# Releasing a weight load by its buffer's last product and by GpSimd's count of scatters

## The chip, the cores and the metric

The kernel runs on one core of a Trainium2 chip. The metric is device time in microseconds (us) of one execution. Three runs of the kernel before took 980.37, 981.39 and 981.79 us, with a median of 981.39.

## The reference

A block of a transformer on 2048 rows of 512 numbers, in float32:

```python
x = x + attention(layernorm(x))   # linear attention, 16 heads of 128, running state
x = x + moe(layernorm(x))         # mixture of experts
```

The change lies in the experts. A classifier scores 64 choices for each row and keeps the best 8. Choices 32 to 63 carry no weights. For each of the 32 real experts, the rows that chose it go through

```python
gu = buf @ w_gate_up[e]           # 512 x 512
g, u = split(gu)
y = (silu(g) * u) @ w_down[e]     # 256 x 512
```

and each result, times the row's weight, is added to that row of the output.

## The kernel before, in words

The kernel has three stages in sequence: `attention`, `routing` (output projection, classifier, and a table of which rows each expert takes) and `experts`. `experts` begins at about 734 us in the profile.

**Weights.** One expert's weights are 1.5 MB, brought in by three DMAs of 512 KB each on SP's queue: the two halves of `w_gate_up` (parts 0 and 1, `load_up`, L1085) and `w_down` (part 2, `load_down`, L1090). A ring of eight buffers (`RING`, L1078) holds eight experts' raw weights; expert e uses buffer e % 8. Experts 0 to 7 are loaded in the stage before and at the start of this one, experts 8 to 31 by the loop at L1191. Products on TensorE are done in pairs of reduced precision, so ScalarE makes a high part of each weight tile (`split_high`, L1114, into `w_h`) and VectorE the rest (`split_low`, L1120, into a low buffer of the same ring place). Both run one to two experts ahead of the products: in step e of their loops (from L1365 and L1432) they split expert e + 2, and for expert e - 5's low part VectorE is therefore in its step e - 7.

**One expert.** GpSimd gathers its rows by an indirect DMA into `m_xg` (`gather`, L1213), two instructions of up to 128 rows each, six experts ahead; TensorE turns them (`turn`, L1254), makes the up product (`up`, L1268), turns the activation (`turn_a`, L1277) and makes the down product (`down`, L1290). In its step e it does `turn_a(e-1)`, `turn(e+1)`, `up(e)`, `down(e-1)` (L1306). ScalarE copies the result into `y`, which has four buffers (`weigh`, L1413); the copy for expert e waits until the scatter of expert e - 4 has landed (L1412). GpSimd adds `y` to the rows of `out` in memory by an indirect DMA (`scatter`, L1223).

**GpSimd's order.** Its loop (L1230) does for each e: the two gathers of expert e + 6 (each waits for VectorE's use of that buffer, L1210), then the scatter of expert e. A scatter waits for the output (L1222) and for the scatter of the expert before it to have landed (L1221). An expert with more than 64 rows has two scatters (the branch at L1237), another has one of 64 rows: 39 scatter instructions in all.

**SP's order.** SP issues loads strictly in order. Before each part of a load for expert e it waits, at L1194, for the last product that reads the buffer (up product of expert e - 8 for parts 0 and 1, its down product for part 2; semaphores `m_gu0`, `m_gu1`, `m_yd0`, `m_yd1`), and at L1195 for VectorE's low part of the same part of expert e - 5 (`m_wl`). After the last load it waits for all scatters (`m_s`, L1200).

`then_inc` raises a semaphore when an instruction is done (for a DMA, when the data has landed); `sem_inc` is an instruction of its own.

Of the kernel before, what the change touches and what calls it, by code (L numbers as in the profile page):

```python
# [1077 lines left out]
RING = 8  # L1078


def load_up(sm, eng, ring, wgu, e, halves=(0, 1)):
    up, _, _, _ = ring[e % RING]
    for i in halves:
        k = slice(2 * i, 2 * i + 2)
        eng.dma_start(up[:, k, :], wgu[e, k].rearrange("k p f -> p k f")).then_inc(sm[f"m_wg{e % RING}"], 16)  # L1085


def load_down(sm, eng, ring, wd, e):
    _, down, _, _ = ring[e % RING]
    eng.dma_start(down, wd[e].rearrange("k p f -> p k f")).then_inc(sm[f"m_wd{e % RING}"], 16)  # L1090
# [32 lines left out]
def experts(nc, sm, wgu, wd, xn2d, out, si, ring, consts, w_h, w_l, v_h):  # L1123


    with ExitStack() as ctx:
# [33 lines left out]
        def flags(eng, name):  # L1160
            return [eng.alloc_register(f"{name}{i}") for i in range(7)]
# [5 lines left out]
        def load_full(eng, regs, e):  # L1167
            eng.reg_load(regs[e % 7], full[0:1, 2 * e:2 * e + 1])  # L1168
# [13 lines left out]
        with nc.Block() as block:  # L1182
            @block.sync
            def _(eng):
                eng.dma_start(ident[:, :], consts[:, 0:128]).then_inc(sm["m_id"], 16)
                eng.wait_ge(sm["m_g01"], 16)
                load_up(sm, eng, ring, wgu, 6)
                load_down(sm, eng, ring, wd, 6)
                eng.wait_ge(sm["m_g11"], 16)
                load_down(sm, eng, ring, wd, 7)  # L1190
                for e in range(RING, NE):  # L1191
                    for part in range(3):
                        for t in range(2):
                            eng.wait_ge(sm[f"m_gu{t}" if part < 2 else f"m_yd{t}"], e - RING + 1)  # L1194
                        eng.wait_ge(sm["m_wl"], 3 * (e - RING + 3) + part + 1)  # L1195
                        if part < 2:
                            load_up(sm, eng, ring, wgu, e, (part,))
                        else:
                            load_down(sm, eng, ring, wd, e)
                eng.wait_ge(sm["m_s"], 32 * NE)  # L1200

            @block.gpsimd
            def _(eng):
                regs = flags(eng, "mp")

                def gather(e, t):

                    i = 2 * e + t
                    if e >= 6:
                        eng.wait_ge(sm[f"m_a{t}"], e - 5)  # L1210
                    else:
                        eng.wait_ge(sm["m_xg"], i + 1)
                    eng.indirect_dma_start(  # L1213
                        xg[:, e % 6, t, :], None, xn2d[:, :],
                        bass.IndirectOffsetOnAxis(ap=si[:, i:i + 1], axis=0),
                        bounds_check=T - 1, oob_is_err=False).then_inc(sm[f"m_g{t}{e % 6}"], 16)

                def scatter(e, t, rows, done):
                    i = 2 * e + t
                    if t == 0 and e >= 1:  # L1220
                        eng.wait_ge(sm["m_s"], 32 * e)  # L1221
                    eng.wait_ge(sm[f"m_y{t}"], e + 1)  # L1222
                    eng.indirect_dma_start(  # L1223
                        out[:, :], bass.IndirectOffsetOnAxis(ap=si[0:rows, i:i + 1], axis=0),
                        y[0:rows, e % 4, t, :], None, compute_op=ALU.add).then_inc(sm["m_s"], done)

                for e in range(6):
                    gather(e, 0)
                    gather(e, 1)
                for e in range(NE):  # L1230
                    if e + 6 < NE:
                        gather(e + 6, 0)
                        gather(e + 6, 1)
                    if e == 0:
                        eng.wait_ge(sm["m_full"], 1)
                    load_full(eng, regs, e)
                    with eng.If_lt(regs[e % 7], T):  # L1237
                        scatter(e, 0, P, 16)
                        scatter(e, 1, P, 16)
                    with eng.Else():  # L1240
                        scatter(e, 0, 64, 32)

            @block.tensor
            def _(eng):
# [197 lines left out]
def build(nc, x, wq, wk, wv, wo, wc, bias, wgu, wd, tabs, ca, cr, out):  # L1442
    with ExitStack() as ctx:
        sm = Sems(nc, ctx)
        oT = nc.dram_tensor("oT", [NC, P, NH, P], F32).ap()
        xn2d = nc.dram_tensor("xn2d", [T, XW], F32).ap()

        with nc.sbuf_tensor("v_h", [P, 24, 512], F32) as v_h, nc.sbuf_tensor("v_l", [P, 24, 512], F32) as v_l:
            pass
        w_h = ctx.enter_context(nc.sbuf_tensor("w_h", [P, 24, 512], F32R))  # L1450
        w_l = ctx.enter_context(nc.sbuf_tensor("w_l", [P, 24, 512], F32R))
        attention(nc, sm, x, wq, wk, wv, wo, tabs, ca, oT, w_h, w_l, v_h, v_l)
        si = ctx.enter_context(nc.sbuf_tensor("si", [P, 64], U32))
        with nc.sbuf_tensor("raw", [P, 18, 512], F32) as raw:
            pass
        low = ctx.enter_context(nc.sbuf_tensor("low", [P, 18, 512], F32R))
        ring = [(v[:, i:i + 4, :], v[:, i + 4:i + 6, :], w[:, i:i + 4, :], w[:, i + 4:i + 6, :])
                for v, w, n in ((raw, low, 3), (v_l, w_l, 4)) for i in range(0, 6 * n, 6)]
        ring7 = ring + [(v_h[:, 20:24, :], None, None, None)]
        routing(nc, sm, x, wo, wc, bias, cr, oT, xn2d, out, si, ring7, wgu, wd, w_h, w_l, v_h, v_l)  # L1460
        experts(nc, sm, wgu, wd, xn2d, out, si, ring, cr, w_h, w_l, v_h)
# [45 lines left out]
```

## Time and profile before

| | us |
|---|---|
| median of three runs | 981.39 |
| the profiled execution | 979.09 |
| its span, first to last instruction | 977.3 |

| engine | busy us | share of the span |
|---|---|---|
| TensorE, products (PE) | 902.5 | 92% |
| VectorE (DVE) | 772.9 | 79% |
| ScalarE (ACT) | 503.3 | 51% |
| GpSimd (POOL) | 482.5 | 49% |

The shares are means over three stages with different limits. The profile counts an instruction that issues an indirect DMA as busy while GpSimd writes its descriptors; the data moves afterwards. SP's DMA issues are listed as SPq, sequencer steps of GpSimd as POOLq.

### The profile page before, as it was taken

How to read it: one execution, taken by the hardware profiler on the slowest of the kernel's cores; microseconds unless marked ns; L12 is line 12 of the kernel's file. 1: busy time of each engine (PE TensorE's matmuls, PEld its weight loads, DVE VectorE, ACT ScalarE, POOL GpSimd, SP SyncE). 2: the span in 40 equal slices, each digit the busy share in tenths (PEclk: the TensorE clock that was granted, in tenths of full speed). 3: DMA queues.
4: the chain of work that ended last, by engine and by line, in shares of the span. 5: the costliest groups of instructions: out<-in, count | busy, mean ns of one | idle time of the engine just before them, and what ended most of it. 6: DMA issues, size and time to landing. Idle time of an engine off the chain costs nothing. (4 is left out here: it accounts for less than half of the span.)

```text
span 977.3 us, 14567 instructions
## 1 busy us (share of the span) xinstructions
PE 902.5 (92%) x4362; PEld 731.1 (75%) x4362; DVE 772.9 (79%) x1843; ACT 503.3 (51%) x867; POOL 482.5 (49%) x395
## 2 busy tenths in 40 slices
PE   4789999999999999999969999999976999998893
PEld 3577888888888888888848888888854677776672
DVE  6978888888888889888977777777776788887670
ACT  5455655555554655554563222332224687876671
POOL 2466766666766667766630000000006456775662
PEclk9999999999999999999999999999998999999897
DMA  8001111111111111110563676443155699999633
GB/s 309 6 33 49 51 46 50 59 45 49 39 59 50 44 59 51 39 59 35 195 224 145 209 266 208 148 148 119 56 192 185 162 331 323 293 299 279 201 43 43
DMA packets 67368, 127.06 MB, mean 130 GB/s; under 512 B 12072, under 2 KB 14504, under 8 KB 65232
## 3 DMA queue, kind: packets, MB, share of 16 engines
q1 hardware_dynamic: 58144, 114.67, 33.7%
q0 software_dynamic: 9136, 11.31, 6.2%
q8 instruction: 43, 0.70, 0.3%
q14 instruction: 45, 0.37, 0.1%
HBM read 106.53 MB, written 32.90 MB: 143 GB/s over the span
## 5 line engine op out<-in xcount | busy, mean ns | idle before, releaser
L595 POOL TENSOR_TENSOR a_t<-a_t 128x512 f32<-128x512 f32 x80 | 105.1, 1314 | 99.0 <-DVE a_t L358 99.0
L604 POOL TENSOR_TENSOR a_fQ<-a_fQ,a_den 128x512 f32<-128x512 f32 x64 | 88.0, 1375 | 71.8 <-DVE a_den L396 71.8
L213 PE MATMUL a_PQ<-w_h,a_xT_h 128*128 128x512 f32 x384 | 106.9, 400 | 10.1 <-DVE w_l L345 9.4
L782 PE MATMUL r_PY<-w_h,r_o_h 128*128 128x512 f32 x256 | 105.9, 414 | 3.4 <-DVE r_o_l L884 3.4
L1070 POOL TENSOR_SCALAR r_vr<-r_mv 128x1 f32<-128x1 f32 x16 | 8.4, 525 | 196.6 <-DVE r_mv L895 196.6
L213 PE MATMUL a_PQ<-w_l,a_xT_h 128*128 128x512 f32 x384 | 104.5, 395 | 0.0
L213 PE MATMUL a_PQ<-w_h,a_xT_l 128*128 128x512 f32 x384 | 103.4, 391 | 0.0
L782 PE MATMUL r_PY<-w_h,r_o_l 128*128 128x512 f32 x256 | 101.0, 395 | 0.0
L1223 POOL DMA_INDIRECT out<-m_y,si x39 | 69.1, 1772 | 64.5 <-DMA out<-m_y,si 51.2
L782 PE MATMUL r_PY<-w_l,r_o_h 128*128 128x512 f32 x256 | 100.5, 393 | 0.0
L392 DVE CUSTOM_DVE_ANT_0 a_m<-a_fQ,a_z 128x128 f32<-128x128 f32 x256 | 100.4, 445 | 0.0
L1213 POOL DMA_INDIRECT m_xg<-xn2d,si x64 | 79.0, 1235 | 39.5 <-DVE m_xg L1340 18.2
L611 POOL TENSOR_TENSOR a_A_l<-a_A,a_A_h 128x512 fp32r<-128x512 f32 x64 | 89.0, 1391 | 6.5 <-ACT a_A_h L480 6.5
L213 PEld LDWEIGHTS a_PQ<-w_h,a_xT_h 128*128 128x128 f32 x384 | 70.0, 190 | 25.3 <-issue 11.2
L357 DVE TENSOR_TENSOR a_t<-a_PQ,a_tab 128x512 f32<-128x512 f32 x80 | 55.0, 688 | 41.7 <-PE a_PQ L213 41.7
L213 PEld LDWEIGHTS a_PQ<-w_l,a_xT_h 128*128 128x128 f32 x384 | 73.2, 191 | 15.8
L494 ACT ACTIVATE a_t<-a_t 128x512 f32<-128x512 f32 x80 | 50.0, 625 | 67.4 <-POOL a_t L595 67.2
L213 PEld LDWEIGHTS a_PQ<-w_h,a_xT_l 128*128 128x128 f32 x384 | 72.9, 190 | 15.4
L480 ACT ACTIVATE a_QT_h<-a_PT 128x512 fp32r<-128x512 f32 x64 | 38.1, 596 | 80.7 <-PE a_PT L221 80.7
L1120 DVE TENSOR_TENSOR w_l<-v_l,w_h 128x1024 fp32r<-128x1024 f32 x48 | 57.2, 1222 | 5.7 <-ACT w_h L1114 4.3
L782 PEld LDWEIGHTS r_PY<-w_h,r_o_h 128*128 128x128 f32 x256 | 48.5, 189 | 12.0 <-issue 3.8
L782 PEld LDWEIGHTS r_PY<-w_h,r_o_l 128*128 128x128 f32 x256 | 48.5, 189 | 11.2
(182 smaller groups left out, 2245.3 us busy)
## 6 DMA issues: line engine op xcount, KB each, us to landing
oT<-a_o SPq DMA_DIRECT2D x64, 256.0 KB, 2.4
v_l<-in_wgu SPq DMA_DIRECT2D x32, 512.0 KB
raw<-in_wgu SPq DMA_DIRECT2D x24, 512.0 KB
v_l<-oT SPq DMA_DIRECT2D x11, 1024.0 KB, 7.2
v_l<-in_wd SPq DMA_DIRECT2D x16, 512.0 KB
raw<-in_wd SPq DMA_DIRECT2D x12, 512.0 KB
v_h<-oT SPq DMA_DIRECT2D x5, 1024.0 KB, 6.9
out<-r_x SPq DMA_DIRECT2D x18, 256.0 KB, 2.0
```

Of the source, the lines that this page charges most:

```text
L213: last = eng.matmul(bank[:, :], a[:, k, :], w[:, 4 * i + k, :], start=s == 0 and k == 0, stop=s == 2 and k == 3)
L357: eng.tensor_tensor(heads(t1[:, r % 2, :]), q, spread(tab[:, c % 2, 0, :]), ALU.mult)
L392: last = eng.tensor_tensor_reduce(m[:, cols], fQ[:, n % 3, cols], z[:, c % 2, g * P:(g + 1) * P], 1.0, 1e-6, ALU.mult, ALU.add, den[:, n % ...
L480: eng.activation(out, in_, ACT.Copy).then_inc(sm[kind], 1)
L494: eng.activation(t2[:, r % 2, :], t1[:, r % 2, :], ACT.Relu, scale=-1.0).then_inc(sm["r"], 1)
L595: eng.tensor_tensor(t1[:, r % 2, :], t1[:, r % 2, :], t2[:, r % 2, :], ALU.add).then_inc(sm["xr"], 1)
L604: eng.tensor_tensor(q, q, den[:, n % 2, :].unsqueeze(2).broadcast_to([P, 4, P]), ALU.mult).then_inc(sm["fs"], 1)
L611: eng.tensor_tensor(A_l[:, n % 2, :], A[:, n % 2, :], f(A_h[:, n % 2, :]), ALU.subtract).then_inc(sm["Al"], 1)
L782: last = eng.matmul(PY[c % 2][:, :], a[:, c % 2, h * P:(h + 1) * P], b[:, h, :], start=h == 0 and s == 0, stop=h == NH - 1 and s == 2)
L1120: eng.tensor_tensor(low, src, high.bitcast(F32), ALU.subtract).then_inc(sm["m_wl"], 1)
L1213: eng.indirect_dma_start(xg[:, e % 6, t, :], None, xn2d[:, :], bass.IndirectOffsetOnAxis(ap=si[:, i:i + 1], axis=0), bounds_check=T - 1, o ...
L1223: eng.indirect_dma_start(out[:, :], bass.IndirectOffsetOnAxis(ap=si[0:rows, i:i + 1], axis=0), y[0:rows, e % 4, t, :], None, compute_op=AL ...
```

## The change

SP no longer waits for VectorE's low part of expert e - 5. From expert 10 on it waits instead until a new semaphore, `m_sent`, has reached e - 9. GpSimd raises `m_sent` by one, by an instruction of its own behind the scatter (or the two scatters) of each expert, so e - 9 is reached behind the scatter of expert e - 10. The waits for the buffer's last product stay.

```diff
                     for part in range(3):
                         for t in range(2):
                             eng.wait_ge(sm[f"m_gu{t}" if part < 2 else f"m_yd{t}"], e - RING + 1)
-                        eng.wait_ge(sm["m_wl"], 3 * (e - RING + 3) + part + 1)
+                        if e >= RING + 2:
+                            eng.wait_ge(sm["m_sent"], e - RING - 1)
                         if part < 2:
                             load_up(sm, eng, ring, wgu, e, (part,))
                         else:
...
                     with eng.If_lt(regs[e % 7], T):
                         scatter(e, 0, P, 16)
                         scatter(e, 1, P, 16)
+                        eng.sem_inc(sm["m_sent"], 1)
                     with eng.Else():
                         scatter(e, 0, 64, 32)
+                        eng.sem_inc(sm["m_sent"], 1)
```

## Rows read from the trace of the kernel before

**Rows 1.** The page, the chain that ended last: shares of the span by line.
```profile
POOL out L1223 1%; POOL m_xg L1213 1%; DMA m_xg<-xn2d,si 1%; PE m_PG L1268 0%; POOLq L1168 0%; POOLq L1182 0%; PE m_PX L1254 0%; DVE m_a L1331 0%; ACT m_s L1401 0%; POOLq L1237 0%; POOLq L1222 0%; POOLq L1213 0%
```

**Rows 2.** The waits, 780 to 880 us: us in total, times, longest us.
```profile
POOL out L1223 <- DMA out<-m_y,si: 20.6, 12, 4.1
```

**Rows 3.** Windows: length, busy us and instructions by engine, TensorE clock, DMA share, GB/s.
```profile
745.00:768.00 23.00, 17.20 (x75) 13.27 (x74) 14.27 (x19) 9.80 (x17) 13.11 (x12) 0.85 0.45 117
780.00:800.00 20.00, 19.11 (x87) 14.05 (x88) 17.62 (x23) 17.40 (x27) 10.96 (x8) 1.00 1.01 334
780.00:880.00 100.00, 95.82 (x449) 73.72 (x450) 84.37 (x106) 82.47 (x126) 69.39 (x45) 1.00 0.98 311
920.00:945.00 25.00, 25.00 (x128) 21.00 (x127) 18.90 (x26) 18.73 (x31) 17.04 (x13) 1.00 0.36 58
```

**Rows 4.** The waits, 880 to 945 us.
```profile
PE m_PX L1254 <- DMA m_xg<-xn2d,si: 6.6, 3, 4.0
```

**Rows 5.** Timeline of POOL, scatters: start us, us, instruction, idle before and its releaser.
```profile
774.41 1.62 POOL L1223 DMA_INDIRECT out<-m_y,si  x1 [5.17 <-ACT m_y L1413]
...
784.95 1.67 POOL L1223 DMA_INDIRECT out<-m_y,si  x1 [4.12 <-DMA out<-m_y,si]
...
804.23 1.47 POOL L1223 DMA_INDIRECT out<-m_y,si  x1 [1.14 <-DMA out<-m_y,si]
...
811.69 1.89 POOL L1223 DMA_INDIRECT out<-m_y,si  x1 [2.83 <-DMA out<-m_y,si]
...
824.06 2.29 POOL L1223 DMA_INDIRECT out<-m_y,si  x1 [0.91 <-DMA out<-m_y,si]
...
831.12 2.22 POOL L1223 DMA_INDIRECT out<-m_y,si  x1 [2.12 <-DMA out<-m_y,si]
...
843.16 1.94 POOL L1223 DMA_INDIRECT out<-m_y,si  x1 [0.30 <-issue]
...
853.54 1.47 POOL L1223 DMA_INDIRECT out<-m_y,si  x1 [2.08 <-DMA out<-m_y,si]
...
860.42 1.99 POOL L1223 DMA_INDIRECT out<-m_y,si  x1 [1.90 <-DMA out<-m_y,si]
...
871.37 2.20 POOL L1223 DMA_INDIRECT out<-m_y,si  x1 [0.74 <-DMA out<-m_y,si]
...
882.25 1.51 POOL L1223 DMA_INDIRECT out<-m_y,si  x1 [2.47 <-DMA out<-m_y,si]
...
895.70 1.63 POOL L1223 DMA_INDIRECT out<-m_y,si  x1 [2.03 <-DMA out<-m_y,si]
...
905.14 1.48 POOL L1223 DMA_INDIRECT out<-m_y,si  x1 [1.68 <-DMA out<-m_y,si]
...
923.93 1.87 POOL L1223 DMA_INDIRECT out<-m_y,si  x1 [2.56 <-DMA out<-m_y,si]
...
950.15 1.76 POOL L1223 DMA_INDIRECT out<-m_y,si  x1 [2.40 <-DMA out<-m_y,si]
...
957.56 1.43 POOL L1223 DMA_INDIRECT out<-m_y,si  x1 [3.77 <-DMA out<-m_y,si]
...
969.18 1.43 POOL L1223 DMA_INDIRECT out<-m_y,si  x1 [2.40 <-DMA out<-m_y,si]
```

**Rows 6.** Timeline of ACT, outputs of experts 5 and 31.
```profile
796.83 0.60 ACT L1413 ACTIVATE m_y<-m_PY 128x512 f32<-128x512 f32 x1
...
962.53 0.60 ACT L1413 ACTIVATE m_y<-m_PY 128x512 f32<-128x512 f32 x1 [2.20 <-PE m_PY L1290]
```

**Rows 7.** Timeline of SP, up loads of experts 8, 18 and 19.
```profile
768.41 1.50 SPq L1085 DMA_DIRECT2D raw<-in_wgu  x2
...
823.94 1.50 SPq L1085 DMA_DIRECT2D raw<-in_wgu  x2
...
832.09 1.50 SPq L1085 DMA_DIRECT2D v_l<-in_wgu  x2
```

**Rows 8.** Timeline of PE, last up product of expert 0.
```profile
746.81 1.07 PE L1268 MATMUL m_PG<-w_h,m_xT_l 128*128 128x512 f32 x4
```

**Rows 9.** The chain in order of time: start us, us, what.
```profile
957.33 0.30 POOLq L1168
```

## The prediction, made before the change was run

> **What bounds the kernel now.** Read the chain of waits first. It names GpSimd's scatter to `out` (L1223) and its gather into `m_xg` (L1213) ahead of everything else, TensorE only behind them [rows 1]. So the expert stage ends on GpSimd, and the waits say what holds GpSimd: between 780 and 880 us its scatters waited 20.6 us, in 12 waits, for the scatter before them to land [rows 2]. `scatter` asks for that (L1221). The windows give the reason: the 16 DMA engines are 98% to 101% busy from 780 to 880 us, at 311 to 334 GB/s, and at 36% and 58 GB/s once the weight loads are over [rows 3]. TensorE waits later, and for GpSimd: 6.6 us in three waits for gathered rows [rows 4].
>
> Now follow GpSimd's scatters [rows 5]. Expert 5's starts at 804.23, expert 22's at 923.93: 17 steps in 119.70 us. Three steps hold two scatters (experts 11, 15, 18: 843.16 to 853.54, 871.37 to 882.25, 895.70 to 905.14: 10.38 + 10.88 + 9.44 = 30.70). The other 14 take 89.00, or 6.36 each. Without loads, from expert 28 to 31, a step takes (969.18 - 957.56) / 3 = 3.87. GpSimd also falls behind: the output of expert 5 is ready at 796.83 + 0.60 = 797.43 [rows 6] and goes out at 804.23; that of expert 31 is ready at 963.13 [rows 6] and goes out at 969.18, 6.05 later.
>
> Last, SP's load issues [rows 7]. Loads are never late for their readers: ScalarE's splits do not appear among the long waits. What a load does to the time is what it does to the scatter beside it.
>
> **The change, part by part.** *Removed:* 72 waits on VectorE's low-part count (3 for each of 24 experts). They paced a load to VectorE's work on the expert five back, whatever GpSimd was doing. What is left of the old condition, the last product out of the buffer, allows expert 8's load when expert 0's second up product is done, at 746.81 + 1.07 = 747.88 [rows 8], where it went at 768.41 [rows 7]: 20.5 us earlier for its first two parts, into a stretch whose DMA engines are 45% busy [rows 3]. The third waits for expert 0's down product as before. I price this by the first step that it uncrowds, expert 1's two scatters to expert 2's, 774.41 to 784.95: 10.54, with 4.12 of waiting at its end [rows 5]. Bounds: 10.54 (no gain), and the two-scatter step without loads, 950.15 to 957.56 = 7.41 (gain 3.13). I take 1.0, near the first end, because loads of experts 9 and 10 still lie beside that step.
>
> *Added on GpSimd:* 32 counts. They are sequencer steps. The step behind a scatter runs at 957.33, before the scatter itself starts at 957.56 [rows 5, 9]: the sequencer passes a scatter as its wait ends, and the count will too, about 0.23 before the scatter starts rather than behind it. The cost is nothing as long as a scatter of 1.43 us or more hides it. Uncovered, at the 0.30 of that step, it would be 32 x 0.30 = 9.6 us.
>
> *Added on SP:* 66 waits (22 experts, three parts). Behind them on SP stand only later loads and the final wait. A load can't become late: `y` has four buffers, ScalarE's copy waits for the scatter four back (L1412), so GpSimd is at most some four experts behind, and a load freed by the scatter ten back still has about four of TensorE's steps before its split. Cost nothing.
>
> *Moved:* from expert 5 or so on, GpSimd's lag (6.8 us there) is more than one step of TensorE, so the count, not the product, comes last. Each load then goes out once per GpSimd step, its first DMA about 0.15 us before a scatter starts (an estimate: the 0.23, less the hop to SP), the other two behind it; SP's issue of two takes 1.50 us [rows 7]. Its bytes are the same, and so is the number of loads between the scatters of experts 5 and 22: 17, one per step. So only their place against the scatter matters.
>
> Its price isn't in the trace; I bound it. Each 512 KB DMA that gets ahead of a scatter costs it 0.524 MB / 334 GB/s = 1.57 us [rows 3]. A step without loads is 3.87. One DMA ahead gives 5.44, two give 7.01. Rows agree with both ends: expert 8's scatter at 824.06, with the load's first DMA 0.12 before it (823.94), made a step of 7.06 to 831.12. Six steps whose load began 0.35 to 0.97 after the scatter (experts 6, 7, 9, 10, 13, 14, of which 832.09 behind 831.12 is one) took 12.37 + 12.04 + 10.95 = 35.36, or 5.89 each [rows 5, 7]. The new place lies between these two patterns: the first DMA is surely ahead, the second is issued just before the 1.43 us of the scatter's own instruction end, the third behind. I take one and a half: 3.87 + 1.5 x 1.57 = 6.22. Against 6.36 that is 14 x 0.14 = 1.9 us.
>
> The two-scatter steps I leave as they are; with loads (10.23 on average) and without (7.41) they differ by 2.8 each, 8.5 in all, which the range takes in. The tail behind expert 22 has no loads in either kernel: 0.
>
> **Sum.** 1.0 + 1.9 = 2.9 us off the profiled execution's 979.09 (span 977.3 and 1.8 around it): 976.2. The median of the runs, 981.39, is 2.3 above that execution, so I predict 978.5. About 0.2% (2 us) is what a measurement of this kernel can tell from no change.
>
> **Floor.** However fast GpSimd becomes, TensorE's chain stays. GpSimd can gain its 6.05 us of lag at the end and TensorE's 6.6 of waiting for rows [rows 4]: 12.7 us, 968.7.
>
> **Rivals.**
> *The scatter keeps ahead.* Steps fall to the 5.89 of the six rows: 14 x 0.47 = 6.5, with the start 7.5 us: 973.9. For it: regular spacing, so that the load before is done when the next begins. Against: the load still goes out before the scatter, which those six did not. Chance 0.30.
>
> *The load gets ahead.* The count is raised as the scatter leaves its wait, SP issues two DMAs before the scatter's own data moves, and every step becomes like expert 8's. Place: the scatter's wait on the scatter before. Price: 14 x (7.01 - 6.36) = 9.1 less 1.0, so slower by 8.1: 989.5. It decides once the second DMA's data precede the scatter's. For it: the 7.06 row, and the 0.23. Against: it is one row, and that scatter's instruction took 2.29 us where a lone one takes 1.43 [rows 5], so that more could slip ahead of it. Chance 0.18.
>
> *Place does not matter.* If the engines served a scatter the same whether a load was issued before or behind it, steps would stay at 6.36, and the start alone would count: 1.0 us off, 980.4. Against: with one load beside each, steps took 5.89 in one pattern and 7.06 in the other. The Trainium skill, page "DMA: Bandwidth & Descriptors", section "Queues, rings and completion order", speaks for this rival and so against the change: each DMA engine takes turns between its queues' rings, packet by packet, so that an earlier issue holds no place in a common line. The two patterns, 1.17 us apart, do not bear that out. Chance 0.08.
>
> *The count is never last*, because GpSimd keeps up: then loads merely go a step earlier, hidden as before: 981.4. The 6.8 us lag is against it. Chance 0.04.
>
> **How the numbers follow.** The forecast, steps of about 6.05 to 6.40, has 0.40: some 975.5 to 981, rather more of it below 979.4 than above (0.25 and 0.15). Faster: 0.25 + 0.30 = 0.55. Within 0.2%: 0.15 + 0.08 + 0.04 = 0.27. Slower: 0.18. The range, 970 to 987, holds the forecast, the rivals at 973.9 and 980.4, and steps up to some 6.8; it leaves out the full price of two DMAs ahead, and gains near the floor.
>
> **What would show it.** In the changed kernel: expert 8's load near 748; from about expert 15 on every load's first DMA 0.1 to 0.7 us before GpSimd's scatter of the expert ten back; steps between scatters more even, near 6.2, and less than 20.6 us of scatter waits from 780 to 880; fewer of TensorE's waits for rows near 890 to 910; last scatter about 3 us earlier, with the same steps of 3.87 behind expert 28. Steps near 7 with more waiting for landings would prove me wrong on the sign, steps near 5.9 on the size. Loads that follow VectorE or TensorE instead of GpSimd's scatters would show that the count isn't what releases them.

## The result, and the profile of the changed kernel

| | before | after |
|---|---|---|
| median of five runs, us | 980.95 | 1000.93 |
| the profiled execution | 979.09 | 996.43 |
| its span | 977.3 | 994.5 |

The ratio is 1.0202, with a 95% interval of 1.0171 to 1.0234: slower, by some 2%, against a forecast of 978.5 and outside its range. The profiled execution is the fastest of the five; what follows is compared with the 977.3 of the span before.

Begin with GpSimd's scatters in the timeline of the changed kernel (start, duration, idle before and its releaser), the rows that answer to [rows 5]: experts 5, 11, 12, 14, 15, 16, 18, 19, 22, 25, 28 and 31. The scatter is now line 1224.

```profile
809.14 2.42 POOL L1224 DMA_INDIRECT out<-m_y,si  x1 [3.51 <-DVE m_a L1334]
...
852.65 1.97 POOL L1224 DMA_INDIRECT out<-m_y,si  x1 [2.87 <-DMA out<-m_y,si]
...
863.57 1.47 POOL L1224 DMA_INDIRECT out<-m_y,si  x1 [3.35 <-DMA out<-m_y,si]
...
876.92 1.48 POOL L1224 DMA_INDIRECT out<-m_y,si  x1 [1.56 <-DMA out<-m_y,si]
...
883.91 2.48 POOL L1224 DMA_INDIRECT out<-m_y,si  x1 [2.10 <-DMA out<-m_y,si]
...
894.13 1.48 POOL L1224 DMA_INDIRECT out<-m_y,si  x1 [2.17 <-DMA out<-m_y,si]
...
909.09 2.55 POOL L1224 DMA_INDIRECT out<-m_y,si  x1 [2.30 <-DMA out<-m_y,si]
...
919.65 1.48 POOL L1224 DMA_INDIRECT out<-m_y,si  x1 [1.68 <-DMA out<-m_y,si]
...
941.36 1.47 POOL L1224 DMA_INDIRECT out<-m_y,si  x1 [2.83 <-DMA out<-m_y,si]
...
956.75 1.65 POOL L1224 DMA_INDIRECT out<-m_y,si  x1 [0.30 <-issue]
...
974.54 1.42 POOL L1224 DMA_INDIRECT out<-m_y,si  x1 [3.35 <-DMA out<-m_y,si]
...
986.26 1.43 POOL L1224 DMA_INDIRECT out<-m_y,si  x1 [2.41 <-DMA out<-m_y,si]
```

From expert 5 to expert 22 the 17 steps take 941.36 - 809.14 = 132.22 us, where they took 119.70. The three steps with two scatters take 10.92 + 10.22 + 10.56 = 31.70 (before 30.70); the 14 single ones 100.52, or 7.18 each (before 6.36). Expert 22 to 31 takes 44.90 (before 969.18 - 923.93 = 45.25). So 12.52 of the 17.2 us arise between experts 5 and 22, none in the tail. The other 4.91 are there at expert 5 already, and 2.50 of those before the first weight split of the stage, which started later in this execution (ScalarE's timeline, the kernel before and the changed one):

```profile
716.07 1.99 ACT L1114 ACTIVATE w_h<-raw 128x1024 fp32r<-128x1024 f32 x2
```

```profile
718.57 1.99 ACT L1114 ACTIVATE w_h<-raw 128x1024 fp32r<-128x1024 f32 x2
```

SP's timeline of the changed kernel shows expert 8's load and, for a step in the middle, expert 24's, which is released by the count behind expert 14's scatter:

```profile
752.57 0.88 SPq L1085 DMA_DIRECT2D raw<-in_wgu  x2
...
876.78 0.88 SPq L1085 DMA_DIRECT2D raw<-in_wgu  x2
877.77 0.41 SPq L1090 DMA_DIRECT2D raw<-in_wd  x1
```

Expert 24's first DMA goes 0.14 us before the scatter at 876.92, its second 0.47 and its third 0.99 behind the first. All three are issued before the scatter's own instruction ends, at 876.92 + 1.48 = 878.40. From expert 15's load on that is so in 15 of 17 steps; in the steps of experts 6 and 8 the third DMA goes as the instruction ends or just behind. In the kernel before, the same two up DMAs took 1.50 [rows 7], not 0.88.

What SP waited for in the changed kernel, 780 to 945 us (us in total, times, longest), shows that the count is what releases the loads:

```profile
SPq L1196 <- POOLq L1244: 91.1, 16, 9.4
SPq L1196 <- POOLq L1241: 16.4, 3, 5.5
```

Next, which bytes move in that step. The DMA view gives packets, MB and share of the engines for each kind of queue: hardware_dynamic holds SP's loads, software_dynamic GpSimd's gathers and scatters. First the changed kernel from 878 to 881 us, then from 881 to 883:

```profile
q1 hardware_dynamic: 478, 0.95, 88.4%
...
q1 hardware_dynamic: 281, 0.54, 72.2%
q0 software_dynamic: 77, 0.13, 35.0%
```

For three microseconds only the load moves, though the scatter's descriptors were written by 878.40. Behind 881 come 0.13 MB of GpSimd's, which is the size of this scatter (64 rows of 2 KB); it lands in time for the next to start at 883.91. Of the load's 1.57 MB, 0.95 go before the scatter's rows and the last of it beside them (0.54 MB between 881 and 883). Where no load is in the way, a scatter's rows move sooner: those of expert 28's, issued at 974.54, between 976.4 and 978 (the DMA view of that stretch):

```profile
q0 software_dynamic: 80, 0.13, 67.0%
```

That is up to 3.5 us behind the scatter's start, where the one at 876.92 has its rows 4.1 to 6.1 us behind it.

The waits of the changed kernel, 780 to 880 and then 880 to 945 us, answer to [rows 2, 4]:

```profile
POOL out L1224 <- DMA out<-m_y,si: 30.9, 12, 4.6
...
PE m_PX L1257 <- DMA m_xg<-xn2d,si: 6.0, 2, 5.3
...
PE m_PX L1257 <- DMA m_xg<-xn2d,si: 10.5, 5, 5.0
ACT m_y L1416 <- DMA out<-m_y,si: 9.9, 3, 5.1
```

Scatters wait 30.9 us for landings where they waited 20.6. GpSimd falls so far behind that others wait for it earlier: TensorE for gathered rows in both stretches (10.5 us in the second, before 6.6), ScalarE's copy for the scatter four back. The windows answer to [rows 3]:

```profile
780.00:880.00 100.00, 90.06 (x409) 68.86 (x409) 78.48 (x98) 75.62 (x113) 57.11 (x41) 0.97 0.85 264
920.00:945.00 25.00, 24.31 (x112) 20.05 (x113) 18.15 (x24) 18.23 (x30) 14.44 (x12) 0.91 0.79 242
```

The DMA engines are 85% busy from 780 to 880 us where they were 98%, and loads still run behind 920 us, where they had run out before. In the kernel before, the engines were full in that stretch; this one is held by a circle: a scatter waits for a load, the next load waits for the next scatter, and the engines idle in between.

### The profile page after: what moved, and what is told of

Read it like the earlier page. It is cut to its first block and busy times, and to the rows that moved or that the text cites. A ratio compares the mean times of both kernels' runs of the same rounds, so it can differ in the third digit from the quotient of the medians.

```text
span 994.5 us, 14599 instructions
## 1 busy us (share of the span) xinstructions
PE 906.7 (91%) x4362; PEld 735.9 (74%) x4362; DVE 773.5 (78%) x1843; ACT 503.7 (51%) x867; POOL 480.1 (48%) x395
## 5 line engine op out<-in xcount | busy, mean ns | idle before, releaser
L1224 POOL DMA_INDIRECT out<-m_y,si x39 | 64.2, 1647 | 80.7 <-DMA out<-m_y,si 64.0
L1214 POOL DMA_INDIRECT m_xg<-xn2d,si x64 | 81.8, 1278 | 40.0 <-DVE m_xg L1343 18.0
L213 PEld LDWEIGHTS a_PQ<-w_h,a_xT_h 128*128 128x128 f32 x384 | 70.1, 190 | 25.4 <-issue 11.3
```

Of the source, the lines that this page charges most:

```text
L213: last = eng.matmul(bank[:, :], a[:, k, :], w[:, 4 * i + k, :], start=s == 0 and k == 0, stop=s == 2 and k == 3)
L1214: eng.indirect_dma_start(xg[:, e % 6, t, :], None, xn2d[:, :], bass.IndirectOffsetOnAxis(ap=si[:, i:i + 1], axis=0), bounds_check=T - 1, o ...
L1224: eng.indirect_dma_start(out[:, :], bass.IndirectOffsetOnAxis(ap=si[0:rows, i:i + 1], axis=0), y[0:rows, e % 4, t, :], None, compute_op=AL ...
```

## The experiments

Theory A: the time follows the number of load DMAs issued ahead of a scatter's own descriptors. Rivals: B, the tie to GpSimd itself, since it lets loads go later; C, the three DMAs come as a burst now that VectorE doesn't pace them, wherever the burst stands; D, late loads starve the splits; E, below.

### None ahead

A small write by GpSimd's engine behind the scatter raises the count, in place of the sequencer's step. `tick` has a column for each expert and is read by nothing. The edit is the same in both branches; one is shown, here and below.

```diff
-                        eng.sem_inc(sm["m_sent"], 1)
+                        eng.memset(tick[:, e:e + 1], 0.0).then_inc(sm["m_sent"], 1)
```

> Edit: the count is raised by a small memset of GpSimd's engine behind the scatter instead of by its sequencer, so that it rises when the scatter's descriptors have been written (some 1.6 us after the scatter's start) and not 0.14 us before it. Everything else is as in the changed kernel. Theory A (three load DMAs issued just ahead of each scatter hold up its landing): the three DMAs are issued at about +1.6, +2.1 and +2.6 us, behind the scatter's own data; the landing is then held by nothing, single steps between scatters fall from 7.18 us towards the 5.3 of the one step of the kernel before whose loads came at +1.72, and the time falls by 14 x (1.3 to 1.9) = 18 to 27 us, to 974 to 983. Theory B (the tie to the scatter itself, which lets loads go late, costs the time): loads go 1.7 us later still, so 1000 or a little more. Theory C (the loads are no longer spaced by VectorE, and a burst of three DMAs in 1 us takes the engines from gathers and scatters wherever it stands): the burst is as dense, so 996 to 1003.

Measured: 974.08 us, ratio to the kernel before 0.9922 (0.9891 to 0.9953). That is 27 us below the changed kernel, with the same releases, some 1.8 us later. Between the two profiles' spans lie 23.4 us: 12.71 in the 14 single steps from expert 5 to 22, 5.82 in the three steps with two scatters, 7.43 before expert 5's scatter, and 2.69 the other way behind expert 22's. The timeline of this kernel around expert 10's scatter, GpSimd first, then SP:

```profile
835.18 1.47 POOL L1225 DMA_INDIRECT out<-m_y,si  x1 [2.40 <-DMA out<-m_y,si]
836.15 0.62 POOL L1245 MEMSET m_tick<- 128x1 f32 x1
...
840.38 1.63 POOL L1225 DMA_INDIRECT out<-m_y,si  x1 [0.30 <-issue]
...
836.85 0.90 SPq L1085 DMA_DIRECT2D v_l<-in_wgu  x2
837.85 0.41 SPq L1090 DMA_DIRECT2D v_l<-in_wd  x1
```

The load goes 1.67 us behind the scatter's start, just behind its end at 836.65. The DMA view of this kernel, 837 to 838.5 and then 839 to 842 us:

```profile
q0 software_dynamic: 75, 0.12, 74.8%
q1 hardware_dynamic: 46, 0.09, 26.2%
...
q1 hardware_dynamic: 555, 1.08, 99.9%
```

Now the scatter's bytes move first and the load's behind them. In the window from 780 to 880 us TensorE is busy 95.66 us again (90.06 in the changed kernel), and the DMA engines 97% (85%):

```profile
780.00:880.00 100.00, 95.66 (x449) 73.90 (x448) 84.79 (x106) 82.89 (x125) 70.34 (x62) 1.00 0.97 293
```

Theories B and C fall as they stand: the tie is the same, the burst is the same (three DMAs within 1.0 us). Single steps took 6.27, not the 5.3 that I expected at best.

### One ahead, two ahead

Both keep the sequencer's count for the first DMA or the first two, and wait for a second semaphore, `m_tick`, raised as above, for the rest. With one ahead:

```diff
-                            eng.wait_ge(sm["m_sent"], e - RING - 1)
+                            eng.wait_ge(sm["m_sent" if part == 0 else "m_tick"], e - RING - 1)
```

With two:

```diff
-                            eng.wait_ge(sm["m_sent"], e - RING - 1)
+                            eng.wait_ge(sm["m_sent" if part < 2 else "m_tick"], e - RING - 1)
```

> Edit: the first of a load's three DMAs waits for the sequencer's count (0.14 us ahead of the scatter), the other two for a count raised by a memset behind the scatter (some 1.6 us after its start). Theory A: one DMA of 0.524 MB instead of three stands ahead of each scatter, so about a third of the way from the kernel with all three behind to the changed one: 982 to 990. Theory B: 998 to 1003. Theory C: the burst is cut in two, 975 to 990, and the same as or faster than the kernel with all three behind.

Measured: 978.85 us, ratio 0.997 (0.994 to 1.000), a little below what A gave.

> Edit: the first two of a load's three DMAs wait for the sequencer's count (ahead of the scatter), the third for a count raised by a memset behind the scatter. Theory A (the time follows the number of load DMAs ahead of the scatter): none ahead gave 974.1, one 978.9, three 1000.9; two lie between, 985 to 994; the rival of the prediction priced two ahead at 989.5. Theory A2 (a threshold: TensorE and the scatters hide one DMA, and any more stands in full): 988 to 1001. Theory C (the density of the burst costs the time): 975 to 982, since the burst is cut in two as with one ahead.

Measured: 990.18 us, ratio 1.0074 (1.0048 to 1.0101). That is in A's span, but also in that of A2, the threshold, so this run does not part the two. From none to three ahead the medians rise by 4.8, 11.3 and 10.8 us: the first DMA costs less than each of the others. SP's timeline with two ahead, beside expert 8's scatter:

```profile
833.69 1.48 POOL L1225 DMA_INDIRECT out<-m_y,si  x1 [1.65 <-DMA out<-m_y,si]
...
833.55 0.88 SPq L1085 DMA_DIRECT2D raw<-in_wgu  x2
835.37 0.37 SPq L1090 DMA_DIRECT2D raw<-in_wd  x1
```

### The write alone

Theory E: the small write helps by itself. Here it stands behind the scatter but raises nothing, and the sequencer's count stays.

```diff
                         eng.sem_inc(sm["m_sent"], 1)
+                        eng.memset(tick[:, e:e + 1], 0.0)
```

> Edit: the changed kernel with its sequencer count, and the same small memset behind the scatter as in the fast kernels, which here raises nothing. Theory A (the place of the loads against the scatter's own descriptors costs the time, and the memset matters only as a later signal): loads stay 0.14 us ahead of a scatter, 996 to 1004. Theory E (the memset itself helps, by holding GpSimd's engine behind the scatter): 970 to 985.

Measured: 999.52 us, ratio 1.0202 (1.0117 to 1.0286). E falls; the write matters as a later signal only.

### The sequencer's count behind the gathers

```diff
                         gather(e + 6, 1)
+                    if e >= 1:
+                        eng.sem_inc(sm["m_sent"], 1)
...
-                        eng.sem_inc(sm["m_sent"], 1)
```

> Edit: the sequencer's count, as in the changed kernel, but raised behind the next expert's two gathers instead of right behind the scatter, with no instruction of GpSimd's engine added. The loads then go some 3 to 4 us behind a scatter's start and 1.5 to 3 us ahead of the next one, so that a part of their 4.7 us still stands ahead of that next scatter. Theory A (what counts is the bytes of load still unfinished ahead of a scatter): better than three DMAs just ahead of it, worse than right behind the last one: 977 to 990. Theory A' (it is the order within the GpSimd queue alone, any place behind the scatter is as good): 970 to 977. Theory D (the sequencer's count is the trouble by itself, wherever it stands): 995 or more.

(D is here another theory than the D above.) Measured: 991.33 us, ratio 1.0092 (1.0054 to 1.013), between A's span and D's. D falls by the kernel with one ahead, which has the sequencer's count too and took 978.85. But the loads did not stand where I had put them. The timeline, the scatters of experts 8 to 10 with the gathers between the first two, and SP's issues behind expert 8's below:

```profile
829.34 1.48 POOL L1224 DMA_INDIRECT out<-m_y,si  x1 [0.56 <-DMA out<-m_y,si]
831.13 1.77 POOL L1214 DMA_INDIRECT m_xg<-xn2d,si  x1 [0.30 <-issue]
833.21 1.00 POOL L1214 DMA_INDIRECT m_xg<-xn2d,si  x1 [0.30 <-issue]
835.28 1.93 POOL L1224 DMA_INDIRECT out<-m_y,si  x1 [1.07 <-DMA out<-m_y,si]
...
842.63 2.09 POOL L1224 DMA_INDIRECT out<-m_y,si  x1 [2.78 <-DMA out<-m_y,si]
...
830.27 0.89 SPq L1085 DMA_DIRECT2D raw<-in_wgu  x2
831.27 0.41 SPq L1090 DMA_DIRECT2D raw<-in_wd  x1
```

The count stands behind two gathers in GpSimd's program, and yet the load that it releases goes at 830.27, before the first of them starts. In most steps it goes 0.93, 1.40 and 1.91 us behind a scatter's start: two DMAs ahead of the end of an instruction of 1.47 us, one behind it; where the instruction runs longer, as that at 835.28 does, all three are ahead. From expert 5 to 21 that makes nine steps with two ahead, seven with three and one with one. So the time is near that of two ahead (990.18), but it is a mean of two kinds: the eight single steps with two ahead took 6.10 on average (829.34 to 835.28: 5.94), the six with three 7.75 (835.28 to 842.63: 7.35), with a scatter instruction 0.69 longer. The prediction's rival in which place does not matter is gone: the same bytes, one per step, at -0.14, +0.93 and +1.67 us give 1000.9, 991.3 and 974.1 us.

### Counted so, these runs fall in order

| load DMAs issued before the scatter's instruction ends | expert 5 to 22, us | median, us |
|---|---|---|
| none: the write behind the scatter | 113.69 | 974.08 |
| one: above | 118.72 | 978.85 |
| two: above | 122.76 | 990.18 |
| two or three: the count behind the gathers | 128.68 | 991.33 |
| three: the changed kernel / with the idle write | 132.22 / 133.17 | 1000.93 / 999.52 |

The single steps in these profiles are 6.27, 6.42, 6.84, 6.81 and 7.18 / 7.31 us.

The count orders bursts, whose DMAs go 0.5 us apart. It does not order the kernel before, where VectorE's wait spaces them by 1.1 us: in seven of its 14 single steps (the prediction's six rows and expert 8's) two DMAs of a load go between 0.12 us before the scatter's start and its instruction's end, the second in six of them only 0.1 us before that end. These seven took 42.42 / 7 = 6.06, not 6.84. So when the DMAs are ahead, their spacing seems to matter too; no run varies it with the place held there.

### VectorE's wait kept beside the count

```diff
                             eng.wait_ge(sm["m_sent"], e - RING - 1)
+                        eng.wait_ge(sm["m_wl"], 3 * (e - RING + 3) + part + 1)
```

> Edit: the wait on VectorE's split is put back beside the count, so each of the three DMAs waits for both. Theory A: the first DMA may still go ahead of the scatter, the others follow VectorE's splits 1.1 us apart or are all already split and go as in the changed kernel; where the spacing comes back single steps are some 6.4 us and the time 980 to 986, where it does not it stays at 1000; the step follows the number of DMAs ahead in each case. Theory B: the release is never earlier than in the changed kernel, so 1000 or more. Theory C: the spacing is back wherever the splits are late, 978 to 984.

Measured: 989.04 us, ratio 1.0099 (1.0057 to 1.0141). Both of A's cases occur in one execution. Up to the scatter of expert 11, VectorE's wait ends last and the first DMA goes 0.57 to 3.41 us behind a scatter's start; from expert 12 on the count ends last, and the three go at -0.09, +0.44 and +0.97. Scatters of experts 5 and 11, then 12 and 15:

```profile
799.24 1.47 POOL L1225 DMA_INDIRECT out<-m_y,si  x1 [0.68 <-DMA out<-m_y,si]
...
836.80 1.63 POOL L1225 DMA_INDIRECT out<-m_y,si  x1 [2.42 <-DMA out<-m_y,si]
...
846.91 2.04 POOL L1225 DMA_INDIRECT out<-m_y,si  x1 [2.83 <-DMA out<-m_y,si]
...
870.42 2.62 POOL L1225 DMA_INDIRECT out<-m_y,si  x1 [3.08 <-DMA out<-m_y,si]
```

Six single steps of 37.56 / 6 = 6.26, then three of 23.51 / 3 = 7.84, in the same kernel. So VectorE's wait did a second service: it held a load's second DMA 1.1 us behind its first. At the scatters of experts 6 to 8 the second went 0.12 us before the scatter's instruction ended (steps of 6.30, 5.90 and 6.27), at the other three both went behind it, and the third DMA of the load before lay within 0.25 us of the scatter's start.

The same wait beside the write's count (and `e - RING - 1` as in the changed kernel):

```diff
+                        eng.wait_ge(sm["m_wl"], 3 * (e - RING + 3) + part + 1)
...
-                        eng.sem_inc(sm["m_sent"], 1)
+                        eng.memset(tick[:, e:e + 1], 0.0).then_inc(sm["m_sent"], 1)
```

> Edit: as in the kernel whose count is raised by a memset behind the scatter, and the wait on VectorE's split is put back beside it. Theory A: every DMA still goes behind the scatter, 1.1 us apart or 0.5; what is lost against the kernel without the split is the earlier start of the loads 8 and 9, for which the prediction took 1.0 us and at most 3.1: 974 to 978. Theory C (spacing the DMAs is worth something of itself): below 972.

Measured: 975.68 us, ratio 0.9905 (0.987 to 0.994). Pacing adds nothing once the place is right. The 1.6 us against 974.08 are no difference: against the kernel before, run beside each, the ratios are 0.9905 and 0.9922, the other way round, and their intervals overlap.

### No count at all

Neither VectorE's wait nor the count: the load goes when its buffer's last product is done.

```diff
-                        if e >= RING + 2:
-                            eng.wait_ge(sm["m_sent"], e - RING - 1)
...
-                        eng.sem_inc(sm["m_sent"], 1)
```

> Edit: neither the wait on VectorE's splits nor the count: a load is released by its buffer's last products alone. Theory A (the place of the loads against the scatter costs the time): each load goes where TensorE's last product falls, some before and some behind a scatter, so a time between the two kernels, 975 to 992, with slow steps exactly where the load lies ahead of the scatter. Theory B (the tie to the scatter): the tie is gone, so 975 to 982. Theory C (an unspaced burst): the burst stays, so 995 to 1003.

Measured: 988.88 us, ratio 1.007 (1.0039 to 1.0102). So the removal of VectorE's wait alone costs some 8 us: TensorE's products put loads at any place of GpSimd's step.

### One expert earlier, one and two later

First the changed kernel with the count of eleven back:

```diff
-                        if e >= RING + 2:
-                            eng.wait_ge(sm["m_sent"], e - RING - 1)
+                        if e >= RING + 3:
+                            eng.wait_ge(sm["m_sent"], e - RING - 2)
```

> Edit: the changed kernel with its sequencer count, but each load waits for the scatter of the expert eleven back instead of ten, so it may go one step earlier at the same place, 0.14 us ahead of a scatter. Theory A: the place is as bad wherever the count comes last, 992 to 1003; where the last products come later than the count the load falls at other places, and the time may be that of the kernel with no count, 985 to 992. Theory D (the release is late): 975 to 984.

Measured: 993.61 us, ratio 1.0101 (1.0067 to 1.0135). The late part of the loads goes 0.14 us ahead of a scatter again, only an earlier one. An earlier release takes some 7 us off the changed kernel, but leaves it slower than the kernel before.

Then the count by the write, with nine back and eight back:

```diff
-                        if e >= RING + 2:
-                            eng.wait_ge(sm["m_sent"], e - RING - 1)
+                        if e >= RING + 1:
+                            eng.wait_ge(sm["m_sent"], e - RING)
```

> Edit: as in the kernel whose count is raised by a memset behind the scatter, but each load waits for the scatter of the expert nine back instead of ten, so it goes one step (some 6 us) later at the same place. Theory A (only the place against the scatter counts, and the loads have room to be late): 972 to 980, steps of 6.0 to 6.4 us. Theory D (later loads starve the splits, which would also have slowed the changed kernel): 984 to 1000, with TensorE or VectorE waiting for weights.

Measured: 971.52 us, ratio 0.9882 (0.9828 to 0.9937).

> Edit: count raised by the memset behind the scatter, each load waiting for the scatter of the expert eight back (the changed kernel: ten; the kernel before this: nine, 971.5). Theory A with room left for late loads: 968 to 976. Theory D (too late for the splits at last): 978 to 995, with TensorE or ScalarE waiting for weights; the early loads 8 and 9 also wait here.

Measured, with eight back (`e >= RING`, `e - RING + 1`): 972.77 us, ratio 0.989 (0.9848 to 0.9932).

> The kernel with the memset's count and the scatter of nine back once more, in five rounds, beside the one with eight back on the same chip: 969 to 975, ratio to the kernel before 0.985 to 0.993.

Measured: 971.41 us, ratio 0.9886 (0.984 to 0.9932). This version beats both kernels: 1.1% below the one before and 29.5 us below the changed one. D falls: loads 6 and 12 us later are still early enough. The waits of nine back (780 to 880, then 880 to 945 us) and its window from 880 to 945:

```profile
POOL out L1225 <- DMA out<-m_y,si: 18.0, 13, 4.5
...
POOL out L1225 <- DMA out<-m_y,si: 10.9, 6, 3.9
```

```profile
880.00:945.00 65.00, 62.92 (x300) 49.34 (x299) 53.55 (x68) 51.06 (x79) 46.79 (x41) 1.00 0.79 216
```

TensorE's wait for gathered rows has left the list of the long waits there, and TensorE is busy 62.92 of the 65 us at a granted clock of 1.00.

## Why the prediction was wrong, step by step

**What bounds the kernel: right.** The scatters' landing and the loads in front of them decide, and the spread of 971 to 1001 us comes mostly from when and where 72 load DMAs are issued.

**When the count rises: right.** I estimated the first DMA 0.15 us before a scatter starts; it goes 0.14 before. That the count ends last once GpSimd lags more than a step was right too.

**How many DMAs get ahead: the step that failed.** I wrote "the first DMA is surely ahead, the second is issued just before the 1.43 us of the scatter's own instruction end, the third behind", because "SP's issue of two takes 1.50 us". Those 1.50 were not SP's. They held a wait for VectorE between the two DMAs, the very wait that the change removes. In the kernel before, VectorE's split and the second up DMA of expert 19, whose first goes at 832.09:

```profile
830.77 2.36 DVE L1120 TENSOR_TENSOR w_l<-v_l,w_h 128x1024 fp32r<-128x1024 f32 x2 [0.25 <-ACT w_h L1114]
...
833.22 0.37 SPq L1085 DMA_DIRECT2D v_l<-in_wgu  x1
```

The second of the two splits ends at 833.13 and the DMA goes 0.09 later. Without the wait the two took 0.88, and the third came 0.99 behind the first. All three are ahead. The row [rows 7] was read as a price of the queue when it was a price of the condition in it.

**What one DMA ahead costs: wrong in base and in slope.** I added 1.57 for each to the quiet step of 3.87. By that, three ahead would take 8.58 a step, and the runs show 7.18 / 7.31; none ahead would take 3.87, and they show 6.27. The 3.87 was measured from expert 28 to 31, where `gather` has no expert left to fetch. In the changed kernel a step with gathers and without loads takes (956.75 - 941.36) / 3 = 5.13 (experts 22 to 25), and at 0.30 of idle it waits for no landing.

The sum also put DMAs behind a scatter at nothing. A scatter has landed at the last update of its semaphore in the trace. In those three steps that is 3.31 to 4.31 us behind its start, but 5.77 on average in the 14 single steps with loads and none ahead: load bytes still move beside its rows. Each DMA ahead then adds (7.18 - 6.27) / 3 = 0.30 us to a single step, as a mean over whole kernels, rather than 1.57. The rise is in the landing: with one, two and three ahead it comes 6.15, 6.57 and 6.91 us behind the start, and the next scatter starts 0.27 behind it. The mean is not a price for every step: it is 0.15 for the first DMA, and in the kernel with the count behind the gathers steps with three ahead are 1.65 longer than steps with two. The rows that seemed to agree with both ends, 5.89 and 7.06, could not part none ahead from one: in all seven steps two DMAs were issued before the scatter's instruction ended.

The errors nearly cancel at two ahead, where the formula says 7.01 and the run 6.84. One and a half ahead, as I had it, lies midway between 978.85 and 990.18, at some 984.5 (an estimate): the forecast of 978.5 would have been too low even with that count.

**Start: not confirmed.** Expert 8's load goes at 752.57, where I had it near 748. Of the 4.91 us that expert 5's scatter is late, 2.41 remain behind the later start of the stage, where I had a gain of 1.0. The loads at -0.14 begin with expert 13's, at the scatter of expert 3, so the lost place acts there already.

**Two-scatter steps, tail, SP's waits:** 31.70 against 30.70, 44.90 against 45.25, and loads that are never late: right for the changed kernel.

**The rivals.** "The load gets ahead" had the mechanism, the place and the sign. It was priced for two DMAs, 989.5; the kernel made for that case gave 990.18, which is luck in part, since the two errors of its price cancel there. The change was the case of three, which neither the rival nor the range held. "The scatter keeps ahead", 973.9, is what a count that is truly behind the scatter gives: 974.08. That the numbers agree is luck: the rival took single steps of 5.89, which were 6.27, and no gain in the steps with two scatters, which fell from 30.70 to 25.88. "Place does not matter", the rival that the Trainium skill, page "DMA: Bandwidth & Descriptors", section "Queues, rings and completion order", speaks for with its turns between rings, is not borne out: 0.95 MB of the load passed in 3 us without a byte of GpSimd's queue between.

## What to carry to other kernels

A semaphore raised by a sequencer's own step did not stand behind the DMA written above it; where a transfer must not get in front of another, raise the signal by an instruction of the engine behind it. Before you remove a wait, ask what it spaces as well as what it guards, and read an issue time that contains a wait as the wait's. A quiet stretch is a base for a sum only if it holds the same work.

## What the runs showed of the hardware that was not expected

**Transfers of two queues went nearly in the order of issue.** SP's loads and GpSimd's scatters lie on different queues. With the load issued before the scatter's instruction ended, only load bytes moved for 3 us; with the load 0.2 us behind that end, the scatter's 0.12 MB moved first. The 1.8 us between the two places are worth 27 us of the kernel's time. Why the engines served them so, no run shows.

**GpSimd's sequencer ran past two gathers that had not started.** With the count behind them, SP's load went at 830.27, 0.86 us before the first gather's instruction and 2.94 before the second.

**The granted clock at the start of the stage was not the same in each execution.** From 745 to 768 us it was 0.99 (nearly all at the upper of its two levels, 2.4 GHz) in the profile with VectorE's wait kept beside the count and 0.72 (over half of it at the lower, 1.2 GHz) in that with the scatter of eight back, with TensorE busy 20.21 and 16.92 us of the 23 (windows of the two):

```profile
745.00:768.00 23.00, 20.21 (x96) 15.80 (x95) 18.15 (x25) 14.29 (x24) 16.44 (x11) 0.99 0.57 153
```

```profile
745.00:768.00 23.00, 16.92 (x64) 13.35 (x63) 13.90 (x20) 7.38 (x14) 12.38 (x12) 0.72 0.42 117
```

Expert 5's scatter stands at 799.24 and 804.00 in these two. A few microseconds at the start of the stage can't be given to an edit by single profiles.
